# A decoder layer on one core: transposes copied a step later in self-attention, the expert plan made at the end of cross-attention

## The reference

```
x = layernorm(x + self_attention(x))      # 16 heads of 32, causal, forget-gate bias, smeared keys
x = layernorm(x + cross_attention(ctx, x, mask))   # 16 heads of 64, keys: ctx (masked) and x
x = layernorm(x + moe(x))                 # 8 experts, the best 2 by router, gelu, 256 -> 1024 -> 256
```

## Time and profile before

| | us |
|---|---|
| median of 3 runs | 2735.02 |
| lowest and highest | 2730.66, 3154.66 |
| the profiled execution | 2734.17 |
| its span, first to last instruction | 2732.4 |
| PE busy | 2407.9 (88%) |
| DVE busy | 1824.2 (67%) |
| ACT busy | 1730.1 (63%) |
| POOL busy | 924.7 (34%) |

### The profile page before, as it was taken

The page is one execution under the profiler, slowest core; times in us unless marked ns, Lnnn a source line. Parts: engine busy times, 40 slices in busy tenths (PEclk is TensorE's granted clock), DMA queues, the critical chain, the costliest instruction groups (busy, mean ns, idle before and its releaser), DMA issues. The chain is left out here.

```text
span 2732.4 us, 60996 instructions
## 1 busy us (share of the span) xinstructions
PE 2407.9 (88%) x17862; PEld 1991.3 (73%) x17862; DVE 1824.2 (67%) x5239; ACT 1730.1 (63%) x4346; POOL 924.7 (34%) x983
## 2 busy tenths in 40 slices
PE   4888888888499999999999999999999469999991
PEld 3666666666377777777777777777776369999991
DVE  5666666667466667666676667666675268888876
ACT  4777787777356566666666666665665256666762
POOL 2434434443423332233322332223321124444434
PEclk9999999999699999999999999999999679999995
DMA  5545445445100000000000000000000157777765
GB/s 122 154 108 123 104 100 123 106 99 118 40 17 17 9 9 16 16 16 1 16 16 16 9 8 16 16 16 9 9 16 9 46 193 232 231 239 234 242 223 192
DMA packets 160229, 224.40 MB, mean 82 GB/s; under 512 B 33872, under 2 KB 127696, under 8 KB 159568
## 3 DMA queue, kind: packets, MB, share of 16 engines
q1 hardware_dynamic: 149040, 201.88, 26.5%
q0 software_dynamic: 9664, 20.53, 2.2%
q10 hardware_dynamic: 1376, 0.54, 0.1%
HBM read 140.15 MB, written 24.01 MB: 60 GB/s over the span
## 5 line engine op out<-in xcount | busy, mean ns | idle before, releaser
L1514 DVE CUSTOM_DVE_ANT_0 x_prob<-x_score,x_mask_add 128x512 f32<-128x512 f32 x512 | 347.9, 682 | 286.7 <-PE x_score L1745 232.0
L1317 ACT ACTIVATE x_prob<-x_prob,x_low 128x512 f32<-128x512 f32 x512 | 366.4, 718 | 190.3 <-DVE x_low L1514 188.0
L1323 ACT COPY x_pt<-x_ptb 128x512 f32<-128x512 f32 x512 | 272.9, 584 | 255.3 <-PE x_ptb L1757 254.7
L1238 POOL TENSOR_TENSOR x_k_lo<-x_whole,x_k_hi 128x512 fp32r<-128x512 f32 x128 | 168.0, 1313 | 413.6 <-ACT x_k_hi L1363 411.2
L1757 PE MATMUL x_ptb<-ident,x_prob 128*128 128x128 f32 x2048 | 267.4, 274 | 2.0 <-PEq L1788 1.8
L1525 DVE TENSOR_SCALAR x_prob<-x_prob,x_rden 128x512 f32<-128x512 f32 x512 | 264.7, 558 | 0.6
L1774 PE MATMUL x_av<-x_pt,x_vx 128*64 128x256 f32 x2048 | 251.0, 387 | 0.8 <-ACT x_pt L1323 0.8
L1757 PEld LDWEIGHTS x_ptb<-ident,x_prob 128*128 128x128 f32 x2048 | 230.4, 141 | 13.8 <-issue 11.1
L484 ACT ACTIVATE prob<-prob,low 128x128 f32<-128x128 f32 (+1 forms) x512 | 229.9, 457 | 5.0 <-DVE low L727 4.8
L1494 DVE COPY x_whole<-x_proj 128x512 f32<-128x512 f32 x192 | 131.0, 688 | 141.7 <-PE x_proj L1678 140.2
L490 ACT COPY pt<-ptb 128x384 f32<-128x384 f32 x258 | 122.4, 474 | 140.5 <-PE ptb L895 140.5
(11 more groups left out here) (274 smaller groups left out, 7283.9 us busy)
## 6 DMA issues: line engine op xcount, KB each, us to landing
w_s<-w SPq DMA_DIRECT2D x156, 512.0 KB, 4.8
k_parts<-k_hi SPq DMA_DIRECT2D x128, 128.0 KB, 2.4
q_parts<-q_hi SPq DMA_DIRECT2D x128, 128.0 KB, 2.4
k_parts<-pos_parts SPq DMA_DIRECT2D x128, 64.0 KB, 2.4
k_parts<-k_lo SPq DMA_DIRECT2D x64, 128.0 KB, 2.4
q_parts<-q_lo SPq DMA_DIRECT2D x64, 128.0 KB, 2.3
w_s<-expert_rows SPq DMA_DIRECT2D x16, 512.0 KB, 4.8
b_s<-b SPq DMA_DIRECT2D x39, 128.0 KB
```

The lines of the kernel that those rows point to most:

```text
L1238: pool.tensor_tensor(part_of(n, q_lo, k_lo), whole_of(n), part_of(n, q_hi, k_hi).bitcast(F32), ALU.subtract).then_inc(low_ready.sem, 1)
L1317: nc.scalar.activation(slot, slot, ACT.Exp, bias=low[:, u:u + 1], scale=-1.0, accum_out=den[:, u:u + 1]).then_inc(exp_ready.sem, 1)
L1323: nc.scalar.copy(pt[:, u % PX_RING, :], ptb[u % 2][:, :]).then_inc(pt_taken[u % 2].sem, 1)
L1514: dve.tensor_tensor_reduce(prob[:, u % PROB_RING, :], score[u % 2][:, :], mask_add[:, :], -X_SCALE, 3.0e38, ALU.add, ALU.min, low[:, u:u + ...
```

## The change

In the self-attention ACT's order within a step changes: after the exponentials come the listed parts, and only then the copy, which is that of head i - 3 (`COPY_LAG` = 3). PE's `transposes` stay at i - 2; `values` moves one step later, since it needs the copies. One more dummy set of transposes ahead of the loop keeps the counts right.

```diff
-    LAG = 2
+    LAG, COPY_LAG = 2, 3
...
-            for s in pt_taken:
-                act.sem_inc(s.sem, (HEADS - LAG) // 2)
+            for n, s in enumerate(pt_taken):
+                act.sem_inc(s.sem, (HEADS - COPY_LAG + 1 - n) // 2)
...
                 for i in range(HEADS):
                     exps(b, i)
-                    take_transposed(*unit(b, i - LAG))
                     for part in parts.get(i, ()):
                         part(b)
+                    take_transposed(*unit(b, i - COPY_LAG))
...
-            for i in range(LAG):
-                take_transposed(*unit(B, i - LAG))
+            for i in range(COPY_LAG):
+                take_transposed(*unit(B, i - COPY_LAG))
...
-            for s, n in ((score_filled, HEADS), (pt_filled, HEADS - LAG),
+            for s, n in ((score_filled, HEADS), (pt_filled, HEADS - COPY_LAG),
...
+            for i in range(3):
+                ins = transpose(ptb[(HEADS - COPY_LAG) % 2][:, i * P:(i + 1) * P], ident[:], ident[:])
+            ins.then_inc(pt_filled.sem, 1)
...
-                g = (i - EC - LAG) // EC
-                if (i - EC - LAG) % EC == 0:
+                g = (i - EC - COPY_LAG) // EC
+                if (i - EC - COPY_LAG) % EC == 0:
                     values(*((b, g) if g >= 0 else (b - 1, g + HPC)))
```

```diff
-            pool.wait_ge(consts, 11)
+            pool.iota(tile_i[:], pattern=[[1, N_TILES]], base=0, channel_multiplier=0).then_inc(consts, 1)
+            pool.iota(bound_i[:], pattern=[[SLOTS, MAX_TILES]], base=0, channel_multiplier=0).then_inc(consts, 1)
+            pool.wait_ge(consts, 13)
+            pool.tensor_copy(tile_no[:], tile_i[:]).then_inc(consts, 1)
+            pool.tensor_copy(bound[:], bound_i[:]).then_inc(consts, 1)
...
             slots_known(B)
             for n in range(TC * TOP):
                 scatter(n)
-            list_extended(B)
...
             dve.tensor_tensor(counts[:], next_free[:], expert_base[:], ALU.subtract).then_inc(counts_ready, 1)
+            dve.wait_ge(counts_ready, 1)
+            step(dve.tensor_tensor(has_tile[:], counts[:].unsqueeze(2).broadcast_to([P, E, MAX_TILES]),
+                                   bound[:].unsqueeze(1).broadcast_to([P, E, MAX_TILES]), ALU.is_gt), 1)
...
+            dve.tensor_copy(tile_base[:], expert_rows_f[:]).then_inc(plan, 1)
...
-            sp.wait_ge(plan, N_PLAN)
             for n in range(RING):
-                load_tokens(Tile(0, n))
                 load_w1(Tile(0, n))
                 load_b1(Tile(0, n))
                 load_w2(Tile(0, n))
+                if n == 0:
+                    sp.wait_ge(scattered.sem, scattered.at(B, scattered.per))
+                    for k in range(RING):
+                        load_tokens(Tile(0, k))
                 if n < 2:
                     load_b2(Tile(0, n))
```

More of the change, by code:

```diff
@@ L985, in _ @@
             one_pass(B - 1, {}, {4: [skips(range(WO))], 9: outputs[:1], 10: outputs[1:], 13: [skips(range(PP, FILLS))]}, False)
-            for i in range(LAG + 1):
+            for i in range(COPY_LAG + 1):
                 if i < LAG:
@@ L1031, in cross_phase @@
         down = sb("down", [P, E])
+        expert_rows_f = sb("expert_rows_f", [P, N_TILES])
+        first_f = sb("first_f", [P, N_TILES])
+        expert_f = sb("expert_f", [P, N_TILES])
+        past_tiles = sb("past_tiles", [P, N_TILES, E])
+        is_past = sb("is_past", [P, N_TILES, E])
+        last_tile = sb("last_tile", [P, E])
+        one_e = sb("one_e", [P, E])
+        tiles_of = sb("tiles_of", [P, E])
+        has_tile = sb("has_tile", [P, E, MAX_TILES])
+        bound = sb("bound", [P, MAX_TILES])
+        bound_i = sb("bound_i", [P, MAX_TILES], I32)
+        tile_no = sb("tile_no", [P, N_TILES])
+        tile_i = sb("tile_i", [P, N_TILES], I32)
         ctx_raw = sb("ctx_raw", [P, TC, D])
@@ L1130, in cross_phase @@
         token_steps = signal("token_steps", 2)
-        counts_ready = sem("counts_ready")
-        N_CONSTS, N_VCONSTS = 14, 3
+        counts_ready, plan = sem("counts_ready"), sem("tile_plan")
+        N_CONSTS, N_VCONSTS = 18, 4
         weights = [(wkv_hi[:, k, :], wkv_s[:, k, :]) for k in range(KC)] + [(wq_hi[:], wq_s)]
@@ L1432, in _ @@
             dve.memset(junk_off[:], float(JUNK)).then_inc(consts_v, 1)
+            dve.memset(one_e[:], 1.0).then_inc(consts_v, 1)
             dve.wait_ge(consts, N_CONSTS)
@@ L1627, in _, with step @@
             dve.tensor_tensor(counts[:], next_free[:], expert_base[:], ALU.subtract).then_inc(counts_ready, 1)
+            def step(ins, n):
+                ins.then_inc(plan, 1)
+                dve.wait_ge(plan, n)
+            dve.wait_ge(counts_ready, 1)
+            step(dve.tensor_tensor(has_tile[:], counts[:].unsqueeze(2).broadcast_to([P, E, MAX_TILES]),
+                                   bound[:].unsqueeze(1).broadcast_to([P, E, MAX_TILES]), ALU.is_gt), 1)
+            step(dve.tensor_reduce(tiles_of[:], has_tile[:], AX_X, ALU.add), 2)
+            step(dve.tensor_tensor_scan(last_tile[:], one_e[:], tiles_of[:], 0.0, ALU.mult, ALU.add), 3)
+            step(dve.tensor_tensor(is_past[:], tile_no[:].unsqueeze(2).broadcast_to([P, N_TILES, E]),
+                                   last_tile[:].unsqueeze(1).broadcast_to([P, N_TILES, E]), ALU.is_ge), 4)
+            step(dve.tensor_tensor(past_tiles[:], is_past[:], tiles_of[:].unsqueeze(1).broadcast_to([P, N_TILES, E]),
+                                   ALU.mult), 5)
+            step(dve.tensor_reduce(expert_f[:], is_past[:], AX_X, ALU.add), 6)
+            step(dve.tensor_reduce(first_f[:], past_tiles[:], AX_X, ALU.add), 7)
+            dve.tensor_scalar(expert_rows_f[:], expert_f[:], float(REGION), None, ALU.mult)
+            step(dve.tensor_tensor(first_f[:], tile_no[:], first_f[:], ALU.subtract), 8)
+            dve.tensor_scalar(tile_expert[:], expert_f[:], float(E - 1), None, ALU.min)
+            step(dve.scalar_tensor_tensor(out=expert_rows_f[:], in0=first_f[:], scalar=float(SLOTS), in1=expert_rows_f[:],
+                                          op0=ALU.mult, op1=ALU.add), 9)
+            dve.tensor_copy(tile_base[:], expert_rows_f[:]).then_inc(plan, 1)
         @block.tensor
@@ L1851, in _, with expert_phase @@
                     skip(B, f)
[L1854 removed]
+def expert_phase(nc, sem, passed, w1, b1, w2, b2, x2_dram, list_dram, out, ident, gates, tile_base, tile_expert, scattered):
     y_dram = nc.dram_tensor("expert_rows", (Y_ROWS + JUNK, D), F32).ap()
@@ L2220, in apart @@
                 dve.sem_inc(passed["dve"], 1)
[L2222 to L2247, removed]
             for s in (xt_taken, y_taken, sum_steps, stats3, ob_ready, *out_stored):
```

38 lines of the change are left out of this document (10 added, 28 removed).

## The result

The changed kernel takes 2690.55 us in the median of four runs (2685.93 to 2693.35), the kernel before 2732.94 (2730.66 to 3154.66): a ratio of 0.9846, with a 95% interval from 0.9824 to 0.9868. One execution of the kernel before, that of 3154.66 us, ran in a slow state, and the ratio leaves it out. The forecast was 2682, its range 2662 to 2712. Its chances were 0.4 for faster by over 2% and 0.56 for a time within 2%, and the latter came. The profiled execution after is the fastest of its four: it took 2685.93 us, its span is 2684.1.

What follows compares the result with a forecast made beforehand. It took self-attention to be bound by an in-order ring of handovers between PE, ACT and DVE. Savings of 48.5 us there and 4.0 us from part 2 took 52.5 off 2734.2, giving 2682 us, range 2662 to 2712.

Steps and rivals of the forecast that it cites:

- Part 1, the mean pass: Self-attention: copies one step later cut the mean pass from 40.73 to 37.5 us, 36.6 without a clock fall.
- the gap ahead of transposes(0): Start of a self-attention pass: PE waits for a copy that ACT makes behind take_xt, a new gap of 2.4 us.
- The clock: PE in self-attention: its clock falls in three passes of five at 1.5 us each, 0.9 us a mean pass.
- rival B: Self-attention: the clock no longer falls, pass 36.6 us, 66 us saved, 2668 us in all; chance 0.22.
- Part 1, over fifteen passes: Self-attention: 3.23 us saved a pass, times 15, 48.5 us in all.
- Part 2, the drain: End of cross-attention: POOL no longer waits for its last four scatters, so the drain begins 1.2 us sooner.
- Part 2, the ramp: Start of the experts' block: weights loaded earlier on SP, 3.2 us saved until PE runs free.
- rival D: Experts' start: tokens behind weights cost what the earlier weights give, self-attention as forecast; 2685 us, chance 0.08.
- The plan: End of cross-attention: twelve DVE instructions move earlier, under the scatters, and count for 0 us there.
- Sum: Whole kernel: 48.5 us from self-attention and 4.0 from the rest, 52.5 off 2734.2, giving 2682 us.
- C: Self-attention: late masked scores or spreads losing their cover let only half arrive; pass 39.1, 2706 us, chance 0.2.
- E: Self-attention: PE held by the ptb bank, old gaps not shrinking; pass 45.0, 64 us slower, 2794 us, chance 0.05.

Runs made afterwards that it cites:

- plan_only: Self-attention of the kernel before, cross-attention and experts of the changed kernel; 2734.85 us, ratio 1.0002 to the kernel before.
- self_only: Self-attention of the changed kernel, cross-attention and experts of the kernel before; 2686.95 us, ratio 0.9828 to the kernel before.
- order_only: Changed kernel with the lag of the copies put back from three heads to two, copy still behind the parts; 2673.06 us, ratio 0.9778 to the kernel before.
- lag_only: Changed kernel with the copy put back ahead of the parts, lag still three heads; 2664.7 us, ratio 0.9747 to the kernel before.
- step1_swap: Changed kernel with the copy ahead of take_xt in step 1 alone; 2662.38 us, ratio 0.9738 to the kernel before.

## Why the prediction came out

**Part 1, the mean pass: right, by two errors that offset each other.** It said 37.5 us, and 37.43 came. The pass without a fall was said to be 36.6 and was 36.22: the gap ahead of transposes(0) was sized at 2.4 us and measured 2.27, output(1) at 1.2 and 1.21, output(0) at 1.5 and 1.15. The waits for xn_lo and tanh_p went. Gaps of 5.0 us are left, where the hand replay had 5.85; PE's own work is 31.2 us (36.22 - 5.04), where the sum had 30.75, since it took 8.5 us of gaps from the old pass and the row shows 7.3 (39.30 - 31.96). The clock was sized too small: three falls in five passes were said, eleven in fourteen came, at the price of 1.5 us that was said. A gap as long as the old one might have been given the old share: a mean pass before carried the whole 1.5 us.

The prediction took the fall for one behind the take_q gap alone. The trace of before has it in four of fourteen passes behind the take_k gap of 1.86 us (in three of these it falls a second time, behind the take_q gap), and that of `plan_only` in three of fourteen. One of them, PE's row and the granted clock behind it:

```profile
353.68 0.39 PE L847 MATMUL proj<-xn_hi,win_hi 128*128 128x256 f32 x1 [1.86 <-DVE k_t L683]
```

```profile
355.30:358.50 3.20, 3.20 (x25) 2.03 (x24) 0.46 (x2) 1.88 (x6) 1.27 (x1) 0.50 0.00 0
```

The Trainium skill (TensorE: Matmul & The Clock Gate, section Why this matters for your kernels) asks for short idle gaps between bursts of matmuls, with a limit longer than any of these. The traces disagree: gaps of 1.86 to 2.34 us lost the clock here. By that limit there would be no fall after the change, and the prediction's sum would be its rival B's 2668 us, an estimate, 14 us lower.

**Part 1, over fifteen passes: 48.5 us said, 47.45 measured in the two traces of the result, 39.6 to 47.5 over all pairs.** That the first pair came so near is in part luck. In it, fourteen intervals give 46.2. The start comes 0.43 us later (55.78 against 55.35), of which the three extra transposes, sized at 0 to 0.4, can be the cause. From the last transposes of x to the block's end it gains 1.7.

**Part 2, the drain: 1.2 us said.** From the end of the last scatter's issue to the experts' opening it was 7.17 us before (7.84 in `self_only`) and 5.88 to 5.89 in all twelve profiles with part 2: 1.3 to 2.0 less. What went is the wait for the scatters. The drain's row is longer now,

```profile
L1020 POOLq DRAIN  x1: 9339/9339/9339, 2109.9 to 2109.9; - x1
```

but it begins ahead of the last scatters' issues and ends at 2119.27, 5.6 us behind the end of the last one (2113.64): those 5.6 us stay, as said.

**Part 2, the ramp: the step that failed.** It said 3.2 us, by "ACT's 2.45 us wait for the second tile's w1 ... is gone, of which 2.1 reach the w2 split" and "so all 3.2 arrive". The wait did go: ACT's second split follows the first within 0.3 us after the change. But ACT's next step, the table load ahead of the gelus, hangs on the first product, and that on the first rows. These came no sooner. The list's load is still issued 5.5 us after the opening, but now behind the loads of the weights, and the gather that waits for it starts 5.4 us after that issue. Before, it started 2.6 us after, and 3.1 in `self_only`, with no weights ahead of it. So the gather is later, 10.9 us after the opening instead of 8.1 and 8.7, and the first product comes at 18.8 where it came at 17.5 before and at 19.3 in `self_only`. That is rival D's mechanism, tokens behind weights, and its price was right too: 4 us of gain fell to about 0 (`plan_only`: 1.0002). I had written that "PE's slow first product holds the gelus", and yet let 2.1 us pass through it. `tokens_first`, which takes the first list out from behind the weights, gained 5.6 us in the block.

**The plan: 0, right.** Its instructions run on DVE from 2108.21 to 2111.95, and the last scatter's issue ends at 2113.63.

**Sum.** Said 52.5 us; the profiled executions differ by 48.3 in span, and the medians by 42.4. Of the first difference 3.15 us are part 2's (-0.85 us over both blocks, -4.0 said) and 1.05 part 1's. The 5.9 us between the two differences are the spread of the executions: the four after the change lie between 2685.93 and 2693.35, and the profiled one is the fastest. By the medians the miss is 10 us: 4 of them are part 2's, and by the ends of the self-attention, 43.2 us apart in the mean where 48.5 were said, some 5 are part 1's.

**The rivals.** B (no fall of the clock, 2668 us) was a state that the ring can have: one copy ahead of `take_xt` gives it, with 2662. C and E did not come: no wait for spreads, no pass above 38. E's mechanism, PE held by the bank, is real, and its first gap measured 2.27 us where 2.4 was said; the old gaps shrank by more.

## What to carry to other kernels

When an in-order engine's ring is shifted by a step, look at both of its edges: the wait that goes, and the buffer's release, which moves behind whatever stands between. One long operation ahead of a release can cost twice, by the gap and by the clock that falls behind it, so try first to break up the longest gap of PE, even where the sum of gaps hardly changes (5.0 to 4.5 us a pass here). And at a block's start put the small load that heads the longest chain, here a list of rows, ahead of the large ones, even where its engine issues it a microsecond earlier at their cost.

## What was not expected of the hardware

- The granted clock is worth more than the gap behind which it falls. The ten falls took 15 us and the gap 3.5. In after, a gap of 2.27 us is followed by a fall in 10 of 13 passes, and in `order_only` one of 2.15 us in 8 of 13; in `lag_only` gaps of up to 1.85 us in 13 passes and in step1_swap of 1.20 us are followed by none. The length of the gap alone does not decide: before, one of 1.86 us was followed by a fall in 4 of 14 passes, and in the first pass one of 1.45 to 1.47 was in after and `self_only` but not in `tokens_first`. What else decides was not tried.
- What a fall costs depends on what follows: 1.5 us in after, 0.5 to 0.8 in `order_only` (36.47 against 37.0 to 37.23). There a pass without a fall has a gap of 1.45 us at take_k, and a pass with one has 0.42: the slower PE uses up a wait that it would have had. The first row is of the pass from 242.73 (no fall), the second of that from 279.20:

```profile
255.10 0.38 PE L852 MATMUL proj<-xn_hi,win_hi 128*128 128x256 f32 x1 [1.45 <-DVE k_t L688]
...
292.20 0.38 PE L852 MATMUL proj<-xn_hi,win_hi 128*128 128x256 f32 x1 [0.41 <-DVE k_t L688]
```

- POOL's drain at the end of the block ends some 5.6 us behind the last thing that POOL did, whether that was a wait for the scatters or the issue of the last one: 5626 ns in `self_only`, where the drain begins behind the wait, and an opening 5.88 us after the last issue in the twelve profiles without the wait.
- What waits for a small load (2 KB) that is issued behind two pairs of weight loads could go on 4.5 to 6.1 us after the load's issue in seven profiles, and 2.6 to 3.1 us after it in the seven with no weights ahead.
